# A graph-network kernel on one core: 64 narrow edge-count windows in place of 32, one incidence tile of four built on ScalarE, VectorE's work in another order

## The chip, the core and the metric

The kernel runs on one core of one Trainium2 chip, in one launch. The metric is the device time of the whole execution in microseconds (us). The engines are TensorE (PE in the profile, its weight loads PEld), VectorE (DVE), ScalarE (ACT), GpSimd (POOL) and SyncE (SP), which only issues transfers. Each engine runs its own program in order, and semaphores tie them together.

## What is computed

A node table x (1024 x 128), 32768 edges (src, dst) sorted by dst, and 64 numbers for each edge. Two layers, each ahead of it a layer norm and a relu:

```python
# layer 1: h = relu(layernorm(x))
nodes_i, nodes_j = h[src], h[dst]
messages = mlp3(concat([nodes_i, nodes_j, edge_attr]))       # 320 -> 256 -> 256 -> 128
summed = segment_sum(messages, src, N) + segment_sum(messages, dst, N)
x = x + mlp3(concat([h, summed, attention(h)]))              # 384 -> 256 -> 256 -> 128
# layer 2: h = relu(layernorm(x)); every node has a loop to itself as well
deg = segment_sum(1, col);  norm = rsqrt(deg)[row] * rsqrt(deg)[col]
out = segment_sum(norm[:, None] * (h @ W)[row], col) + b
x = x + gelu(out)
```

## The kernel before, in words

**Edges.** 32768 edges are 256 tiles of 128 edges, or 64 groups of 4 tiles. All stages of a group run in a software pipeline: in its step g each engine works on parts of the groups g - 1, g and g + 1. `run_groups` writes out the steps -1 to 64, one after the other, on each engine.

**TensorE, step g** (`group`, L677 to L698): `second_layer(g, 0)` and `second_layer(g, 1)` (L607, 6 matmuls of 512 columns each), `first_layer(g + 1)` (L587, 4 matmuls for the edge numbers, then L593, for each half k four transposes that add the gathered rows to the two banks), between its halves `scatter(g - 1, 0)` (L628, 4 matmuls), `messages(g)` (L617), and `scatter(g - 1, 1 to 3)` (L628). The transposes of tiles 0 and 1 in the first half wait for the first `add_pair` of VectorE, those of tiles 2 and 3 for the second. `scatter` multiplies the messages (high and low part) with an incidence matrix `inc` (128 edges x 1024 nodes), so that both segment sums of the reference come in one product.

**The incidence matrix** of a tile is |node - (src + dst)/2| == |src - dst|/2, times 2 for a loop edge. ScalarE's `distance` (L812) writes the left side to `dist` (f16), VectorE's `incidence` (L1005) compares and writes `inc` (fp32r). For tiles 0 and 2 (`IN_ROWS`) both have the shape of 3 rows of 342 on one side, for 1 and 3 one run of 1024.

**GpSimd** gathers for every tile one row per edge from each of two tables (L446, L454), 8 transfers for a group, into one of 3 buffers. VectorE adds the two in pairs of tiles (`add_pairs`, L1048).

**High and low parts.** After each product ScalarE writes the rounded high part (`relu_first` L796, `high_messages` L819, `round_edges` L825), and VectorE the rest (`low_first` L985, `low_messages` L991, `low_edges` L979). `relu_second` is L802 on ScalarE.

**Edge counts for layer 2.** `ct_sb` (1024 x 1024 counts) is made in `NW` = 32 windows of `WD` = 32 target nodes. As dst is sorted, a window's edges lie in a few tiles: `VT` = 10 are always done. For each of them VectorE writes two one-hot matrices, `oh_low` (L1056, 128 columns) and `oh_key` (L1057, 258 columns as 3 rows of 86 at a pitch of 88), and TensorE multiplies them (L646, `count_tile`, put between the transposes). A window takes two groups, 5 tiles in each. Then ScalarE copies it to `ct_sb` (L853, `window_out`), and VectorE sums it in both directions (`window_sums`, L1076, L1078). What a window has beyond 10 tiles is added by `more_windows`, a loop that always makes one visit; it stands ahead of step 63 on VectorE and within it on TensorE. After it come `count_ends` (L664), `degrees` and `add_bias_of_sums` (L672). GpSimd adds the diagonal of the loops last (L479).

**VectorE, step g** (`group`, L1008 to L1038): one-hots 0 and 1; `incidence(g - 1, 1)`; both pair sums; one-hot 2; `incidence(g - 1, 2)`; `low_edges`; `low_first(g + 1, 0)`; `incidence(g - 1, 3)`; one-hot 3; `low_first(g + 1, 1)`; one-hot 4; `incidence(g, 0)`; `low_messages(g)`; in even steps `window_sums`.

**ScalarE, step g** (L827 to L848): `round_edges(g + 2)`, `relu_second(g, 0)`, `distance(g - 1, 2)`, `relu_second(g, 1)`, `relu_first(g + 1, 0)`, `distance(g - 1, 3)`, `relu_first(g + 1, 1)`, `distance(g, 0)`, `high_messages(g)`, `distance(g, 1)`, in even steps `window_out`.

## Time and profile before

| | us |
|---|---|
| median of 3 runs | 767.0 (766.85 to 767.35) |
| the profiled execution | 765.72 |
| its span | 763.9 |

```profile
PE 736.0 (96%) x4171; PEld 619.3 (81%) x4171; DVE 729.5 (96%) x1506; ACT 524.3 (69%) x711; POOL 539.0 (71%) x533
PE   7589999999999999999999999999999999999896
DVE  7889999999999999999999999999999999999775
```

The first line is each engine's busy time, its share of the span, and its number of instructions. The other two cut the span into 40 slices: a digit is the busy share in tenths, and 9 is 90% or more. TensorE and VectorE are full from the third slice on to the last four. TensorE had its full clock in nearly all of the span (mean 0.994).

### The profile page before, as it was taken

The numbers are of one execution on the slowest core, as the hardware profiler recorded it, in microseconds if no ns is written. First come the engines' busy times: TensorE is split into PE (matmuls) and PEld (weight loads), VectorE is DVE, ScalarE is ACT, GpSimd is POOL, SyncE is SP. The second block draws the span as 40 slices with busy tenths as digits, with TensorE's granted clock in tenths as the row PEclk, the third lists the DMA queues.
The fourth block names the chain that finished last, engine by engine and source line by source line (L and its number), as shares of the span: only waits on it lengthen the run. The fifth ranks groups of instructions, "written<-read, shape, count | busy, mean of one in ns | idle before, by whom it ended". The sixth has DMA issues, their size and how long they took to land.

```text
span 763.9 us, 13342 instructions
## 1 busy us (share of the span) xinstructions
PE 736.0 (96%) x4171; PEld 619.3 (81%) x4171; DVE 729.5 (96%) x1506; ACT 524.3 (69%) x711; POOL 539.0 (71%) x533
## 2 busy tenths in 40 slices
PE   7589999999999999999999999999999999999896
PEld 6467888888888888888888888888888888888755
DVE  7889999999999999999999999999999999999775
ACT  3256777777777777777777777777777777776623
POOL 3777777777777777777777777777777777777100
PEclk9899999999999999999999999999999999999999
DMA  7534444344434444344443444434443444432000
GB/s 227 164 119 129 128 127 123 117 126 129 126 112 125 130 128 127 114 124 128 127 124 113 130 129 126 126 112 127 129 126 113 126 127 130 126 111 83 0 1 28
DMA packets 42566, 90.15 MB, mean 118 GB/s; under 512 B 11136, under 2 KB 17920, under 8 KB 42496
## 3 DMA queue, kind: packets, MB, share of 16 engines
q0 software_dynamic: 24576, 67.14, 28.6%
q1 hardware_dynamic: 17920, 22.16, 9.9%
q8 instruction: 33, 0.54, 0.3%
q14 instruction: 37, 0.30, 0.1%
HBM read 86.64 MB, written 2.62 MB: 117 GB/s over the span
## 4 chain that ended last, share of the span: by engine, by line
PE 88%; DVE 4%; POOL 3%; issue 2%; DMA 2%; ACT 1%; DVEq 0%; SPq 0%; POOLq 0%
PE bank L628 30%; PE bank L607 22%; PE bank L617 14%; PE bank L587 7%; PE bank L593 7%; PE bank L646 4%; POOL rows_sb L446 2%; POOL rows_sb L454 1%; DVE ring L1005 1%; PE bank L720 1%; DMA w_sb<-mW 1%; PE bank L765 1%; PE bank L728 1%; DMA table_a<-rows_sb 0%; PE bank L714 0%
## 5 line engine op out<-in xcount | busy, mean ns | idle before, releaser
L446 POOL DMA_INDIRECT rows_sb<-table_a,ends_i x256 | 263.5, 1029 | 82.2 <-issue 77.7
L454 POOL DMA_INDIRECT rows_sb<-table_b,ends_i x256 | 262.7, 1026 | 78.0 <-issue 78.0
L812 ACT ACTIVATE dist<-iota_h,neg_mid 128x1026 f16<-128x1026 f16 (+1 forms) x256 | 292.3, 1143 | 0.0
L1005 DVE TENSOR_SCALAR ring<-dist,half_gap,times 128x1026 fp32r<-128x1026 f16 (+1 forms) x256 | 276.4, 1081 | 1.7 <-ACT dist L812 0.6
L628 PE MATMUL bank<-ring,m_hi 128*128 128x512 f32 x512 | 172.4, 418 | 1.3 <-DVE ring L1005 1.1
L802 ACT ACTIVATE h_sb<-bank,b_sb 128x512 f32<-128x512 f32 x128 | 87.6, 684 | 122.5 <-PE bank L607 122.5
L628 PE MATMUL bank<-ring,m_lo 128*128 128x512 f32 x512 | 160.8, 395 | 0.0
L607 PE MATMUL bank<-ring,w_hi 128*128 128x512 f32 x512 | 150.0, 394 | 1.4 <-DVE ring L985 1.4
L1057 DVE TENSOR_SCALAR oh_key<-iota_h,key_f,minus_base 128x258 bf16<-128x258 f16 x321 | 128.5, 400 | 0.0
L617 PE MATMUL bank<-w_sb,h_sb 128*128 128x128 f32 x1024 | 124.8, 275 | 0.0
L593 PE MATMUL bank<-ident,rows_sb 128*128 128x128 f32 x512 | 113.7, 276 | 8.0 <-DVE rows_sb L1048 8.0
L617 PEld LDWEIGHTS bank<-w_sb,h_sb 128*128 128x128 f32 x1024 | 119.5, 192 | 0.1
L796 ACT ACTIVATE ring<-bank 128x512 fp32r<-128x512 f32 x128 | 76.7, 599 | 60.1 <-PE bank L593 55.8
L607 PEld LDWEIGHTS bank<-ring,w_hi 128*128 128x128 f32 x512 | 96.1, 188 | 24.4 <-DVE ring L985 2.0
L628 PEld LDWEIGHTS bank<-ring,m_lo 128*128 128x128 f32 x512 | 96.9, 189 | 23.2
L628 PEld LDWEIGHTS bank<-ring,m_hi 128*128 128x128 f32 x512 | 87.2, 191 | 13.9 <-DVE ring L1005 2.0
L985 DVE SCALAR_TENSOR_TENSOR ring<-bank,ring 128x512 fp32r<-128x512 f32 x128 | 87.8, 686 | 3.7 <-ACT ring L796 1.7
L593 PEld LDWEIGHTS bank<-ident,rows_sb 128*128 128x128 f32 x512 | 70.3, 142 | 20.7 <-DVE rows_sb L1048 11.2
L1056 DVE TENSOR_SCALAR oh_low<-iota_h,low_f 128x128 bf16<-128x128 f16 x321 | 84.8, 264 | 2.2 <-issue 2.1
L1048 DVE TENSOR_TENSOR rows_sb<-rows_sb 128x512 f32<-128x512 f32 x128 | 82.2, 681 | 3.7 <-DMA rows_sb<-table_b,ends_i 3.6
L607 PE MATMUL bank<-ring,w_lo 128*128 128x512 f32 x256 | 80.3, 395 | 0.0
L646 PE MATMUL bank<-oh_key,oh_low 128*128 128x258 bf16 x320 | 77.8, 275 | 0.0
(182 smaller groups left out, 628.5 us busy)
## 6 DMA issues: line engine op xcount, KB each, us to landing
e_raw<-edge_attr_t SPq DMA_DIRECT2D x128, 128.0 KB, 3.1
rows_sb<-table_a,ends_i POOLq DMA_INDIRECT x256, 2.8
rows_sb<-table_b,ends_i POOLq DMA_INDIRECT x256, 2.9
table_a<-rows_sb SPq DMA_DIRECT2D x4, 256.0 KB, 3.4
table_b<-rows_sb SPq DMA_DIRECT2D x4, 256.0 KB, 2.5
x_sb<-x SPq DMA_DIRECT2D x2, 256.0 KB, 3.2
out<-oh_key SPq DMA_DIRECT2D x4, 128.0 KB, 1.8
u_sb<-uW SPq DMA_DIRECT2D x1, 384.0 KB, 5.0
```

Of the source, the lines that this page charges most:

```text
L446: nc.gpsimd.indirect_dma_start(got[:, b, t, 0, :], None, table_a, bass.IndirectOffsetOnAxis(ap=ends_i[:, 0, tile:tile + 1], axis=0),).then ...
L454: nc.gpsimd.indirect_dma_start(got[:, b, t, 1, :], None, table_b, bass.IndirectOffsetOnAxis(ap=ends_i[:, 1, tile:tile + 1], axis=0),).then ...
L593: mm = nc.tensor.matmul(z1t_bank[k][:, t * P:(t + 1) * P], got[:, g % GB, t, 0, part], ident[:, :], start=False, stop=True, is_transpose=T ...
L607: mm = nc.tensor.matmul(z2_bank[m][:, :], w[:, k, m * P:(m + 1) * P], a[:, b, k, :], start=(n == 0), stop=(n == len(parts) - 1))
L617: mm = nc.tensor.matmul(msg_bank[:, t * D:(t + 1) * D], h2_sb[:, k, t * P:(t + 1) * P], w3_sb[:, k, :], start=(t == 0 and k == 0), stop=(k ...
L628: mm = nc.tensor.matmul(acc_bank[n][:, :], part[:, b, t, :], inc[:, t, n * HB:(n + 1) * HB], start=(is_first(g) and t == 0 and part is m_h ...
L646: mm = nc.tensor.matmul(bank[2][:, 0:KR * KN], oh_low[:, w % HOT, j, :], oh_key[:, w % HOT, j, :, 0:KN], start=(j == 0), stop=(j == VT - 1 ...
L802: nc.scalar.activation(h2_sb[:, m, :], z2_bank[m][:, :], ACT.Relu, bias=b2_sb[:, m:m + 1]).then_inc(h2_ready, 1)
L812: nc.scalar.activation(to, of, ACT.Abs, bias=neg_mid[:, bass.ds(g * GT + t, 1)]).then_inc(dist_ready, 1)
L985: nc.vector.scalar_tensor_tensor(h1_lo[:, b, k, :], z1t_bank[k][:, :], 0.0, h1_hi[:, b, k, :].bitcast(F32), ALU.max, ALU.subtract).then_in ...
L1005: nc.vector.tensor_scalar(to, of, half_gap[:, tile], times[:, tile], ALU.is_equal, ALU.mult).then_inc(inc_ready, 1)
L1057: return nc.vector.tensor_scalar(oh_key[:, slot, j, :, 0:KN], iota_h[:, 0:KR * KN].rearrange("p (r n) -> p r n", r=KR), key_f[:, bass.ds(t ...
```

## The change

- `VT` 10 to 6, `NW` 32 to 64, `WD` 32 to 16: 6 tiles to a window, one window to a group. `oh_key` is 2 rows of 64 at a pitch of 66 (128 columns), `HOT` 2 to 4 slots. TensorE does the 6 products together, between the second half of `first_layer` and `messages`. Steps -1, 0 and 1 make two windows each (12 tiles), after `low_messages`, so nothing is made ahead of step -1.
- Two windows are a pair. VectorE adds a pair to `ct_sb` (`pair_out`, in place of ScalarE's copy) and sums it (`pair_sums`), in every other step.
- `ct_sb` is cleared by ScalarE at the start (8 instructions of 1024 columns), with the diagonal copied in (2 more), in place of GpSimd's additions at the end. `more_windows` stands ahead of the steps, behind a wait for these 10. `count_ends` and `degrees` go from step 63 to step 62.
- Incidence tile 3 is made on ScalarE by three instructions: `distance`, `last_gap` (Abs), `last_incidence` (Relu), but for the last group's. Tiles 0, 1 and 2 are all in rows, but for the last group's.
- VectorE's pair sums, one-hots and incidence tiles stand in another order, and so do ScalarE's instructions.
- The bias rows (L474 on GpSimd) are added by VectorE in step 0. In the last step TensorE adds the bias of the sums first and does one half of the columns after the other.

```diff
-    VT = 10
-    NW = 32
+    VT = 6
+    NW = 64
-    KR, KN, KP = 3, 86, 88
+    KR, KN, KP = 2, 64, 66
-    HOT = 2
+    HOT = 4
-    IN_ROWS = (0, 2)
+    IN_ROWS = (0, 1, 2)
+    DT = GT - 1
...
+        FILL = 2
+        def made_in(g):
+            if g < FILL:
+                return [2 * (g + 1), 2 * (g + 1) + 1]
+            return [w for w in (g + 2 + FILL,) if w < NW]
+        def counted_in(g):
+            if 0 <= g <= FILL:
+                return [2 * g, 2 * g + 1]
+            return [w for w in (g + 1 + FILL,) if FILL < g and w < NW]
+        def summed_in(g):
+            pairs = [p for p in range(PAIRS) if 2 * p + 1 in counted_in(g - 1)]
+            return pairs[0] if pairs else None
+        LAST_SUM = NW - 1 - FILL
...
+            def count_window(w):
+                pe.wait_ge(w_hot, w + 1)
+                if w % 2 == 0:
+                    wait(pe, w_out, w // 2)
+                at = (w // 2) % 2 * PK + w % 2 * WK
+                for j in range(VT):
+                    mm = nc.tensor.matmul(bank[2][:, at:at + WK], oh_low[:, w % HOT, j, :], oh_key[:, w % HOT, j, :, 0:KN],
+                                          start=(j == 0), stop=(j == VT - 1), skip_group_check=True)
+                mm.then_inc(w_psum, 1)
+            def last_scatter(g, b):
+                pe.wait_ge(m_lo_ready, g + 1)
+                for n in range(NH):
+                    for t in range(GT):
+                        if n == 0:
+                            wait_incidence(g, t)
+                        for part in (m_hi, m_lo):
+                            mm = nc.tensor.matmul(acc_bank[n][:, :], part[:, b, t, :], inc[:, t, n * HB:(n + 1) * HB], ...
+                    mm.then_inc(sums_ready, 1)
             def group(g, b, i):
+                if g == GROUPS:
+                    add_bias_of_sums()
+                    last_scatter(g - 1, 1 - b)
+                    return
                 if nxt:
-                    first_layer(g + 1, 1 - b, i + b, 1, counts_of(g))
+                    first_layer(g + 1, 1 - b, i + b, 1)
+                for w in counted_in(g):
+                    count_window(w)
                 if now:
                     messages(g)
-                if g == LAST_W + 1:
+                if g == LAST_SUM + 1:
                     count_ends()
...
+            def clear_counts(chunks):
+                for c in chunks:
+                    nc.scalar.activation(ct_sb[:, c, :], iota_h[:, 0:N], ACT.Copy, scale=0.0).then_inc(ct_zero, 1)
+            def last_gap(g):
+                act.wait_ge(dist_ready, GT * g + GT)
+                nc.scalar.activation(dist[:, DT, 0:N], dist[:, DT, 0:N], ACT.Abs,
+                                     bias=neg_gap[:, bass.ds(g * GT + DT, 1)]).then_inc(gap_ready, 1)
+            def last_incidence(g):
+                act.wait_ge(gap_ready, g + 1)
+                wait(act, scattered, GT * g)
+                tile = bass.ds(g * GT + DT, 1)
+                nc.scalar.activation(inc[:, DT, 0:N], dist[:, DT, 0:N], ACT.Relu, bias=times[:, tile],
+                                     scale=neg_times[:, tile]).then_inc(last_inc_ready, 1)
             # ScalarE, step g
+                if past:
+                    distance(g - 1, 2)
                 if now:
                     relu_second(g, 0)
                 if past:
-                    distance(g - 1, 2)
+                    distance(g - 1, 3)
                 if now:
                     relu_second(g, 1)
+                if past and now:
+                    last_gap(g - 1)
                 if nxt:
                     relu_first(g + 1, 1 - b, 0)
-                if past:
-                    distance(g - 1, 3)
+                if past and now:
+                    last_incidence(g - 1)
                 if nxt:
                     relu_first(g + 1, 1 - b, 1)
...
             # VectorE, step g, as it is after the change
+                if steady:
+                    w = makes[0]
+                    tile0 = window_tile(w)
+                    one_hots(w, tile0, (0,))
+                if nxt:
+                    add_pair(g + 1, 0)
                 if past:
                     incidence(g - 1, 1)
+                if nxt:
+                    add_pair(g + 1, 1)
+                if pair is not None:
+                    pair_out(pair)
                 if past:
                     incidence(g - 1, 2)
+                if steady:
+                    one_hots(w, tile0, (1,))
+                if nxt:
+                    low_first(g + 1, 1 - b, 0)
                 if exists(g + 2):
                     low_edges(g + 2, b)
                 if nxt:
                     low_first(g + 1, 1 - b, 1)
+                if steady:
+                    one_hots(w, tile0, (2,))
+                if pair is not None:
+                    pair_sums(pair)
+                if steady:
+                    one_hots(w, tile0, (3,))
                 if now:
                     incidence(g, 0)
+                if steady:
+                    one_hots(w, tile0, (4, 5))
+                if now:
                     low_messages(g, b)
+                if not steady:
+                    for w in makes:
+                        one_hots(w, window_tile(w), range(VT))
+                if g == 0:
+                    biased_rows()
+                if g == GROUPS:
+                    incidence(g - 1, 3)
...
+            def pair_out(p):
+                dve.wait_ge(w_psum, 2 * p + 2)
+                counts = ct_sb[:, :, bass.ds(p * PD, PD)]
+                found = bank[2][:, p % 2 * PK:(p % 2 + 1) * PK].rearrange("p (d a) -> p a d", a=NC)
+                nc.vector.tensor_tensor(counts, counts, found, ALU.add).then_inc(w_out, 1)
             def more_windows():
-                dve.wait_ge(w_sums, NW)
+                dve.wait_ge(ct_zero, NC + 2)
```

## Rows read from the trace of the kernel before

**Rows 1.** Busy time by stretch: us, PE, PEld, DVE, ACT, POOL, clock, DMA, GB/s.
```profile
300.00:400.00 100.00, 100.00 (x582) 85.43 (x581) 99.16 (x196) 74.09 (x100) 77.15 (x76) 1.00 0.40 123
```

**Rows 2.** Timeline, TensorE, step 34: start us, us, engine, line, op, count.
```profile
403.11 0.62 PE L607 MATMUL bank<-ring,w_hi 128*128 128x512 f32 x2
...
406.82 0.27 PE L593 MATMUL bank<-ident,rows_sb 128*128 128x128 f32 x1
...
406.93 0.27 PE L646 MATMUL bank<-oh_key,oh_low 128*128 128x258 bf16 x1
...
407.15 0.25 PEld L593 LDWEIGHTS bank<-ident,rows_sb 128*128 128x128 f32 x2
...
409.19 1.95 PE L617 MATMUL bank<-w_sb,h_sb 128*128 128x128 f32 x16
...
413.78 0.62 PE L607 MATMUL bank<-ring,w_hi 128*128 128x512 f32 x2
```

**Rows 3.** Timeline, ScalarE, step 34; in brackets its idle time before and who ended it.
```profile
404.70 0.69 ACT L802 ACTIVATE h_sb<-bank,b_sb 128x512 f32<-128x512 f32 x1 [2.05 <-PE bank L607]
...
405.29 1.14 ACT L812 ACTIVATE dist<-iota_h,neg_mid 128x1026 f16<-128x1026 f16 x1
...
407.68 0.60 ACT L796 ACTIVATE ring<-bank 128x512 fp32r<-128x512 f32 x1 [0.67 <-PE bank L593]
```

**Rows 4.** Groups of instructions by shape: busy us, mean ns, idle before.
```profile
L454 POOL DMA_INDIRECT rows_sb<-table_b,ends_i x256 | 262.7, 1026 | 78.0 <-issue 78.0
...
L1005 DVE TENSOR_SCALAR ring<-dist,half_gap,times 128x1026 fp32r<-128x1026 f16 x128 | 170.5, 1332 | 0.3 <-ACT dist L812 0.3
...
L1057 DVE TENSOR_SCALAR oh_key<-iota_h,key_f,minus_base 128x258 bf16<-128x258 f16 x321 | 128.5, 400 | 0.0
...
L1056 DVE TENSOR_SCALAR oh_low<-iota_h,low_f 128x128 bf16<-128x128 f16 x321 | 84.8, 264 | 2.2 <-issue 2.1
...
L1076 DVE TENSOR_REDUCE into_part<-ct_sb 128x32 f32<-128x256 f32 x32 | 19.3, 602 | 0.1
L1078 DVE TENSOR_REDUCE from_part<-ct_sb 128x8 f32<-128x256 f32 x32 | 13.1, 409 | 0.0
```

**Rows 5.** Timeline, VectorE, step 23.
```profile
291.03 0.69 DVE L979 TENSOR_TENSOR e_parts<-e_raw,e_parts 64x512 fp32r<-64x512 f32 x1
291.75 0.69 DVE L985 SCALAR_TENSOR_TENSOR ring<-bank,ring 128x512 fp32r<-128x512 f32 x1
...
294.63 1.33 DVE L1005 TENSOR_SCALAR ring<-dist,half_gap,times 128x1026 fp32r<-128x1026 f16 x1
295.88 0.68 DVE L991 TENSOR_TENSOR m_lo<-bank,m_hi 128x512 fp32r<-128x512 f32 x1
```

**Rows 6.** Timeline, start: ScalarE's last L861, VectorE's first sum of pairs.
```profile
26.35 0.69 ACT L861 ACTIVATE uh_sb<-bank,ub_sb 128x512 f32<-128x512 f32 x1 [0.76 <-PE bank L571]
...
33.70 1.29 DVE L1048 TENSOR_TENSOR rows_sb<-rows_sb 128x512 f32<-128x512 f32 x2
...
43.46 0.69 DVE L1048 TENSOR_TENSOR rows_sb<-rows_sb 128x512 f32<-128x512 f32 x1 [2.92 <-DMA rows_sb<-table_b,ends_i]
```

**Rows 7.** Chain that ended last, in order of time: step 4's second layer.
```profile
83.19 2.80 PE bank L607 x12
```

**Rows 8.** Timeline, end: TensorE from step 63 on.
```profile
712.69 0.63 PE L607 MATMUL bank<-ring,w_hi 128*128 128x512 f32 x2
...
720.86 1.84 PE L664 MATMUL bank<-ones_col,into_part 128*128 128x1 f32 x16
...
727.80 0.74 PE L628 MATMUL bank<-ring,m_hi 128*128 128x512 f32 x2 [1.14 <-DVE ring L1005]
...
732.30 3.70 PE L714 MATMUL bank<-rows_sb,u_sb 128*128 128x512 f32 x8 [0.24 <-ACT rows_sb L870]
```

**Rows 9.** Timeline, VectorE, the one visit of `more_windows`.
```profile
714.16 0.23 DVE L1096 TENSOR_SCALAR over_f<-rows_f,visit_f 1x32 f32<-1x32 f32 x1 [1.19 <-issue]
...
718.67 0.41 DVE L1120 TENSOR_TENSOR ct_sb<-ct_sb,bank 128x256 f32 x1
```

More of the change, by code:

```diff
@@ L804, in distance @@
             def distance(g, t):
-                wait(act, inc_ready, GT * g + (t - 3))
+                if t < DT:
+                    wait(act, inc_ready, DT * (g - 1) + t + 1)
+                else:
+                    wait(act, last_inc_ready, g)
                 to, of = dist[:, t, 0:N], iota_h[:, 0:N]
-                if t in IN_ROWS:
+                if t in IN_ROWS and g < GROUPS - 1:
                     to = dist[:, t, :].rearrange("p (r n) -> p r n", r=DR)[:, :, 0:DN]
@@ L862, in _ @@
                                      bias=ub1_sb[:, m:m + 1]).then_inc(uh_ready, 1)
+            clear_counts(range(NC - 2, NC))
+            act.wait_ge(ct_zero, NC)
+            act.wait_ge(consts_pool, 7)
+            diagonal = ct_all[:, 0:(NC - 1) * (N + P)].rearrange("p (s n) -> p s n", n=N + P)[:, :, 0:P]
+            nc.scalar.copy(diagonal, ident[:, :].unsqueeze(1).broadcast_to([P, NC - 1, P])).then_inc(ct_zero, 1)
+            nc.scalar.copy(ct_all[:, (NC - 1) * (N + P):NC * N], ident[:, :]).then_inc(ct_zero, 1)
             nc.scalar.copy(w1e_hi[:, :], w1e_sb[:, :]).then_inc(w1e_hi_ready, 1)
@@ new lines, in group, with biased_rows, add_pair @@
+                if g == 0:
+                    biased_rows()
+                if g == GROUPS:
+                    incidence(g - 1, 3)
+            def biased_rows():
+                dve.wait_ge(ld_w, 16 * 12)
+                nc.vector.tensor_tensor(xb_sb[:, :, :], x_sb[:, :, :],
+                                        ub3_all[:, :].unsqueeze(1).broadcast_to([P, NC, D]), ALU.add).then_inc(xb_ready, 1)
+            def add_pair(g, half):
+                b, n = g % GB, g // GB
+                tiles = slice(2 * half, 2 * half + 2)
+                for t in (2 * half, 2 * half + 1):
+                    dve.wait_ge(ga_done[b][t], 16 * (n + 1))
+                    dve.wait_ge(gb_done[b][t], 16 * (n + 1))
+                nc.vector.tensor_tensor(got[:, b, tiles, 0, :], got[:, b, tiles, 0, :], got[:, b, tiles, 1, :],
+                                        ALU.add).then_inc(pair_added, 1)
@@ L1203, in _ @@
             dve.wait_ge(rows_ready, 1)
+            more_windows()
             dve.wait_ge(w1e_hi_ready, 1)
@@ L1207, in _ @@
             low_edges(0, 0)
-            tile0 = window_tile(0)
-            for half in range(2):
-                one_hots(0, tile0, half, range(VT // 2))
-            run_groups(dve, group, FIRST + 1, {1: count_passes, LAST_W: more_windows, LAST_W + 1: degrees})
+            run_groups(dve, group, FIRST + 1, {1: count_passes, LAST_SUM: sum_counts, LAST_SUM + 1: degrees})
             def round_counts(chunks):
```

157 lines of the change are left out of this document (52 added, 105 removed).

## Prediction

> **What bounds the kernel now.** I read the busy time by stretch first. In the middle of the run, all 100 us of a stretch of 100 us are busy on TensorE and 99.2 on VectorE, with ScalarE at 74 and GpSimd at 77, at full clock [rows 1]. So two engines share the bound, and the timelines have to say which sets the pace. On TensorE the second layer of step 34 starts at 403.11 and that of step 35 at 413.78 [rows 2]: 10.67 us for a step. Between these rows I saw no gap longer than the usual one from instruction to instruction, and the list of waits has none for TensorE in the middle. VectorE's instructions stand just as close, and ScalarE waits 2.05 us for TensorE ahead of L802 [rows 3]. So TensorE sets 10.67 and VectorE follows with almost no slack. What takes work from both can gain only if no chain through several engines is longer than a step. That chain is what I cost below. Times within a step count from the start of its second layer (step 34: 403.11).
>
> **Prices.** A VectorE instruction starts 0.08 before the one ahead of it ends (294.63 + 1.33 is 295.96, and the next starts at 295.88 [rows 5]). So an incidence tile in rows costs 1.25, a pair sum or a low part 0.60, L979 0.72 (291.03 to 291.75 [rows 5]), L1056 some 0.17, L1057 of 258 columns 0.32, and the two window reduces 0.52 + 0.33 = 0.85 [rows 4]. On ScalarE the overlap is 0.10 (404.70 + 0.69 against 405.29 [rows 3]), so a distance costs 1.04, L802 0.59, L796 0.50.
>
> **TensorE's own step.** It loses 5 count products at 0.11 each (406.82 to 406.93 [rows 2]), 0.54. It gains 6 of 128 columns. Bounds for one: 0.11 if the columns don't matter, 0.054 if they all do (128/258 of 0.109). I take 0.055, since the pitch of the 258-column product is just 258 columns long, which leaves no sign of a fixed part: 0.33. The own step becomes 10.67 - 0.54 + 0.33 = 10.46, or 10.79 by the upper bound. (The Trainium skill, page "TensorE: Matmul & The Clock Gate", section "Back-to-back issue gap", gives 81 ns for a stream of 128-column products with their weight loads. No row here shows one. By it the step would be 10.62, and it speaks against the change.)
>
> **VectorE's own step.** The narrower L1057 has the 128 columns of L1056. Its pitch lies between 0.17 (that row's) and 0.32 (no change). I take 0.21, near the lower end, since only one scalar operand sets it apart: a one-hot costs 0.38, bounds 0.34 and 0.49. Two steps hold 6 incidence tiles 7.50, 4 pair sums 2.40, 4 `low_first` 2.40, 2 `low_edges` 1.44, 2 `low_messages` 1.20, 12 one-hots 4.56, `pair_out` 0.33 (256 elements like L1078) and the reduces 0.85: 20.7, or 10.3 a step. It has slack of its own. (By "VectorE: DVE Perf Modes", section "What auto-detection actually checks" of the Trainium skill, two ports serve an instruction if the outermost counts of both sides are even or equal. The old L1057 writes 3 rows and doesn't qualify, the new one writes 2 and does. That agrees with a shorter L1057, but those ports are shared with GpSimd, see the fourth rival.)
>
> **ScalarE** gets two more instructions of 1.04 a step and loses half of L853. It was 74% busy [rows 1], that is 7.9 us of a step, so it goes to some 9.8 and fits. But it does the new work ahead of results others wait for.
>
> **The chain.** Second layer starts at 0; L802 starts at 1.59 (404.70 [rows 3]); then, in program order, distance 3 at 2.18, `relu_second` 1 at 3.22, `last_gap` 3.81, `relu_first` 0 at 4.85, `last_incidence` 5.35, `relu_first` 1 at 6.39 to 6.99. (Before, `relu_first` 0 started at 4.57 [rows 3], set by the transposes.) The new instructions are bounded by 0.9 and 1.15 each; I take the distance's 1.04. Then VectorE goes on with `low_first` 1: 0.60, one-hot 0.38, reduces 0.85, one-hot 0.38, incidence 0 1.25, two one-hots 0.76, `low_messages` 0.60, in the next step one-hot 0.38, pair sum 0.60, incidence 1 1.25, second pair sum 0.68: 7.73, end at 14.7. The transposes of tiles 2 and 3 wait for that sum. Their weights were loaded at 407.15, 4.04 into the step [rows 2]; without two counts ahead of them it is 3.82, so 3.82 + 10.46 = 14.28 in the next step. The sum comes 0.45 late and TensorE stands. From there it needs 10.46 - 3.82 = 6.64 to the next second layer, at 21.4. In the step without reduces the sum ends 0.85 earlier and is in time. Two steps take 21.4, one takes 10.69, against 10.67 before. So the 0.21 that TensorE's own step gains is eaten, and what is late next is the second pair sum. With the bounds for counts and one-hots the step is 10.6 to 11.1.
>
> **The start.** Ahead of step -1 stood 10 one-hots (4.8 us, up to the first pair sum at 33.70 [rows 6]). Now `more_windows` stands there, behind ScalarE's clears. The last L861 starts at 26.35 [rows 6]; two clears and two diagonal copies (1.04 twice, an estimated 1.2 for both copies) end at 30.3. The visit costs 1.19 of issue, 714.16 to 718.67, less two reduces of 0.34, plus 0.41 [rows 9] and 0.3 to its end: 5.7. With L1205 (0.4) and L979 VectorE is free at 37.0, not at 33.7, and the second layer of step 0 starts at about 42.5 (it takes 5.5 from there, at a clock that has fallen while TensorE idled; a guess of 0.5 either way). Then VectorE carries 12 one-hots (4.55) in each of the steps -1, 0 and 1 where it had 5. In order: step -1 ends on it at 47.0; step 0 (pair sums 1.2, a wait of 1.1 for ScalarE, low parts 2.0, incidence and `low_messages` 1.85, one-hots 4.55, bias rows 1.15) at 58.9; step 1 (13.3, and 1.1 for `count_passes`) at 73.4; step 2, with a pair, at 84.4; the second pair sum of step 3 at 87.3. So step 4's second layer starts at 94.0, where it was 83.19 [rows 7]: **10.8 late**. Before, VectorE had waited here for gathers (2.92 us at 43.46 [rows 6]), which is gone as cover now: GpSimd is ahead by then. Bounds: 8 (one-hot 0.34, visit 5) to 14.
>
> **The middle.** 56 steps from 4 to 60 at +0.02: +1. Steps 60 to 62 have no one-hots on VectorE and run at TensorE's own 10.46, 10.13 and 10.13 + 1.79 for `count_ends` (L664, 16 matmuls, 1.84 with its tail [rows 8]). That is 32.5 against some 32.3: +0.2, with 0.4 more for the disturbed step 62 of before. I count +0.6, so step 63 starts 12.4 later than at 712.69 [rows 8].
>
> **The end.** Before, from 712.69 to the update's first matmul at 732.30 [rows 8] it was 19.6, with the visit, `count_ends`, a wait of 1.14 for incidence and the bias behind. Now from 0: second layer to 2.8, scatter to 3.7, messages 3.9 to 5.7, scatter to 8.5, bias 1.0 to 9.5. ScalarE's distance 3 of the last group ends at 10.8 and VectorE's fast tile at 11.6; then 10 matmuls of 0.235 after it: 14.0. So **-5.6**. The two edits that cost nothing here: the order of halves (it only lets ScalarE copy earlier) and the diagonal, which ScalarE does in the start.
>
> **Sum**, against the profiled execution's own 765.7: +10.8 + 1.0 + 0.6 - 5.6 = +6.8, 772.5. The median of the runs shown lies 1.3 higher, so I forecast 773.8, **774**.
>
> **The rivals.** About 0.2% is what a measurement of this kernel can tell from no change.
> 1. *TensorE's own step sets the pace* (faster). If the chain is shorter than 20.9 instead of 21.4 (one-hots at 0.34 give 0.2, new ScalarE instructions at 0.9 give 0.4), the 56 steps run at 10.46: 56 x 0.21 = 11.8 less than at 10.67, and 774 - 12.9 = 761. For it: two engines get less work. Against: VectorE's order, with reduces between `low_first` 1 and the pair sums. It decides from a chain of 20.9 on, and is in sight for all below 21.2. Chance 0.22.
> 2. *The count products cost as much as before*, 0.11: the part behind the pair sum grows by 0.33, two steps take 21.7, 56 x 0.16 more, 783. Against: the pitch follows columns elsewhere. Chance 0.12.
> 3. *The start costs half*: if the clears are through early or the long one-hot runs fit into waits, 4 to 6 us less, 769, or 767 with a chain a little shorter. Chance 0.12.
> 4. *GpSimd becomes the bound.* A gather takes 1.026 + 0.30 [rows 4], 8 of them 10.6 a step, with VectorE's fast instructions in their way. The fast incidence tiles go, 7 short one-hot instructions come. Only above 10.9 a step would it matter, since it is a buffer or two ahead: 785 at 10.9. Chance 0.04.
>
> **How the numbers follow.** The forecast has 0.50, on 770 to 780. Slower by over 0.2%: forecast 0.50, rivals 2 and 4 0.16, a part of 3, together 0.70. Within 0.2%: 0.08, from 3. Faster: 0.22. The range reaches from rival 1 to rival 2: 760 to 784.
>
> **What would show it.** In the changed kernel's profile: TensorE waits at L593 for the pair sum in every other step, 0.3 to 0.6 each time, and two steps take 21.2 to 21.6; the second layer of step 4 starts near 94; VectorE has a wait ahead of `low_first` in steps with a pair; count products follow each other by 0.055; the update starts 14 us after step 63. Wrong would be: no wait on TensorE in the middle (rival 1), or a step 4 that starts below 90.

## The result, and the profile after

| | before | after |
|---|---|---|
| median, us | 766.92 (4 runs) | 782.06 (4 runs, 781.32 to 783.39) |
| the profiled execution | 765.72 | 781.32 |
| its span | 763.9 | 779.6 |
| ratio of the medians, 95% interval | | 1.020 (1.018 to 1.022) |

The kernel got 15.1 us slower; I had forecast 6.8 slower, with 784 as the upper end of the range. The page of the kernel after, busy time and slices:

```profile
PE 737.6 (95%) x4235; PEld 617.2 (79%) x4235; DVE 725.4 (93%) x1601; ACT 645.7 (83%) x815; POOL 539.6 (69%) x530
PE   7486999999999999999999999999999999999996
DVE  7689999999999999999999999999999999998665
PEclk9878999999999999999999999999999999999999
```

Two places show already. In slices two to four TensorE is at 4, 8 and 6 tenths and its granted clock at 8, 7 and 8, and in the middle, by stretch (the view of [rows 1]), TensorE is no longer full:

```profile
300.00:400.00 100.00, 98.82 (x574) 83.47 (x574) 97.85 (x211) 89.83 (x112) 77.31 (x75) 1.00 0.42 124
```

TensorE's timeline over two steps, the counterpart of [rows 2]:

```profile
421.00 0.63 PE L611 MATMUL bank<-ring,w_hi 128*128 128x512 f32 x2
...
425.38 0.44 PE L599 MATMUL bank<-ident,rows_sb 128*128 128x128 f32 x2 [0.27 <-DVE rows_sb L1112]
...
427.02 0.50 PE L651 MATMUL bank<-oh_key,oh_low 128*128 128x128 bf16 x6
427.36 2.00 PE L621 MATMUL bank<-w_sb,h_sb 128*128 128x128 f32 x16
...
431.97 0.63 PE L611 MATMUL bank<-ring,w_hi 128*128 128x512 f32 x2
...
442.51 0.63 PE L611 MATMUL bank<-ring,w_hi 128*128 128x512 f32 x2
```

One step takes 10.97 and the next 10.54, and in the longer one the transposes of tiles 2 and 3 wait for the second sum of pairs (L1112). The six count products take 0.34 together. The chain that leads to this wait starts one step earlier, in the step with the reduces (TensorE and VectorE):

```profile
410.47 0.63 PE L611 MATMUL bank<-ring,w_hi 128*128 128x512 f32 x2
...
417.54 0.69 DVE L1029 SCALAR_TENSOR_TENSOR ring<-bank,ring 128x512 fp32r<-128x512 f32 x1 [0.20 <-ACT ring L821]
...
424.64 0.68 DVE L1112 TENSOR_TENSOR rows_sb<-rows_sb 128x512 f32<-128x512 f32 x1
```

Here `low_first` 1 starts 7.07 after the second layer, the second sum of the next step ends 7.78 after that (425.32), and 6.65 later the next second layer starts (431.97). ScalarE in the longer step (the counterpart of [rows 3]):

```profile
422.60 0.69 ACT L827 ACTIVATE h_sb<-bank,b_sb 128x512 f32<-128x512 f32 x1 [0.97 <-PE bank L611]
423.19 1.14 ACT L840 ACTIVATE dist<-iota_h,neg_mid 128x1024 f16<-128x1024 f16 x1
424.22 0.68 ACT L827 ACTIVATE h_sb<-bank,b_sb 128x512 f32<-128x512 f32 x1
424.79 1.14 ACT L846 ACTIVATE dist<-dist,neg_gap 128x1024 f16<-128x1024 f16 x1
425.86 0.60 ACT L821 ACTIVATE ring<-bank 128x512 fp32r<-128x512 f32 x1
426.35 1.23 ACT L855 ACTIVATE ring<-dist,times,neg_times 128x1024 fp32r<-128x1024 f16 x1
427.48 0.59 ACT L821 ACTIVATE ring<-bank 128x512 fp32r<-128x512 f32 x1
```

That is the order of the forecast's chain; `last_incidence` (L855) has a pitch of 1.13 where I had 1.04. The list of waits of the kernel after (us in total, times, the longest):

```profile
PEld bank L599 <- DVE rows_sb L1112: 25.0, 32, 4.7
DVE ring L1029 <- ACT ring L821: 17.3, 45, 2.4
```

Where the time lies, by the start of each step's second layer:

| | before | after | change |
|---|---|---|---|
| step 4 | 83.03 | 97.78 | +14.75 |
| steps 4 to 60 | 597.45 (10.669 a step) | 603.35 (10.774) | +5.9 |
| steps 60 to 63 | 32.21 | 32.72 | +0.5 |
| step 63 to the end of the span | 51.2 | 45.73 | -5.4 |

The start, by stretch (the columns of [rows 1]), in the kernel after:

```profile
37.00:43.00 6.00, 4.00 (x13) 3.12 (x14) 3.55 (x7) 1.70 (x3) 4.53 (x5) 0.50 0.47 139
43.00:48.00 5.00, 5.00 (x12) 3.88 (x13) 5.00 (x25) 0.69 (x1) 3.78 (x5) 0.50 0.51 159
...
61.00:66.00 5.00, 3.84 (x16) 2.93 (x17) 4.62 (x6) 1.76 (x3) 4.09 (x4) 0.53 0.27 78
```

From 43 to 48 TensorE was busy all the time at a granted clock of 0.50, the lower level of 1.2 GHz: it had idled 8.25 us up to 34.76 and 2 us each up to 37.0 and 42.76. The second layer of step 0 took 5.3 us there, where that of step 34 took 2.8. (Up to step 4 the clock was at 0.50 from 32 to 48, from 59 to 65 and from 80 to 82; in the kernel before from 32 to 38 alone.) After an idle time of 4.3 us up to 60.96 the clock was at 0.53 again. The end went as the forecast had it: the update's first matmul comes 14.2 after step 63, where it was 19.6 after it [rows 8].

### The profile page after: what moved, and what is told of

Same layout as the page of the kernel before. It is cut to its first block, busy times and chain, and to the rows that moved or that the text cites. A ratio compares the mean times of both kernels' runs of the same rounds, so it can differ in the third digit from the quotient of the medians.

```text
span 779.6 us, 13796 instructions
## 1 busy us (share of the span) xinstructions
PE 737.6 (95%) x4235; PEld 617.2 (79%) x4235; DVE 725.4 (93%) x1601; ACT 645.7 (83%) x815; POOL 539.6 (69%) x530
## 4 chain that ended last, share of the span: by engine, by line
PE 68%; DVE 21%; issue 6%; ACT 3%; DVEq 1%; POOL 0%; POOLq 0%
PE bank L639 25%; PE bank L621 14%; PE bank L611 12%; PE bank L599 7%; DVE ring L1049 5%; DVE rows_sb L1112 5%; PE bank L593 4%; DVE oh_low L1120 3%; PE bank L651 3%; DVE oh_key L1121 2%; DVE m_lo L1035 2%; ACT dist L840 1%; PE bank L737 1%; PE bank L782 1%; ACT ring L821 1%
## 5 line engine op out<-in xcount | busy, mean ns | idle before, releaser
L470 POOL DMA_INDIRECT rows_sb<-table_b,ends_i x256 | 272.6, 1065 | 78.0 <-issue 78.0
L462 POOL DMA_INDIRECT rows_sb<-table_a,ends_i x256 | 260.0, 1016 | 82.7 <-issue 77.4
L1049 DVE TENSOR_SCALAR ring<-dist,half_gap,times 128x1026 fp32r<-128x1026 f16 (+1 forms) x193 | 255.5, 1324 | 6.3 <-ACT dist L840 6.2
L1121 DVE TENSOR_SCALAR oh_key<-iota_h,key_f,minus_base 128x128 bf16<-128x128 f16 x385 | 131.7, 354 | 0.0
L621 PE MATMUL bank<-w_sb,h_sb 128*128 128x128 f32 x1024 | 128.1, 278 | 0.1
L1029 DVE SCALAR_TENSOR_TENSOR ring<-bank,ring 128x512 fp32r<-128x512 f32 x128 | 88.2, 689 | 21.2 <-ACT ring L821 17.3
L599 PE MATMUL bank<-ident,rows_sb 128*128 128x128 f32 x512 | 85.4, 281 | 16.9 <-DVE rows_sb L1112 16.9
L1120 DVE TENSOR_SCALAR oh_low<-iota_h,low_f 128x128 bf16<-128x128 f16 x385 | 99.1, 258 | 1.8 <-issue 1.8
L599 PEld LDWEIGHTS bank<-ident,rows_sb 128*128 128x128 f32 x512 | 64.7, 144 | 42.8 <-DVE rows_sb L1112 25.0
L639 PEld LDWEIGHTS bank<-ring,m_hi 128*128 128x128 f32 x504 | 86.2, 191 | 11.3
L1112 DVE TENSOR_TENSOR rows_sb<-rows_sb 128x512 f32<-128x512 f32 x128 | 87.0, 681 | 0.0
L855 ACT ACTIVATE ring<-dist,times,neg_times 128x1024 fp32r<-128x1024 f16 x63 | 78.0, 1238 | 0.0
```

Source lines behind the costliest of these rows:

```text
L462: nc.gpsimd.indirect_dma_start(got[:, b, t, 0, :], None, table_a, bass.IndirectOffsetOnAxis(ap=ends_i[:, 0, tile:tile + 1], axis=0),).then ...
L470: nc.gpsimd.indirect_dma_start(got[:, b, t, 1, :], None, table_b, bass.IndirectOffsetOnAxis(ap=ends_i[:, 1, tile:tile + 1], axis=0),).then ...
L599: mm = nc.tensor.matmul(z1t_bank[k][:, t * P:(t + 1) * P], got[:, g % GB, t, 0, part], ident[:, :], start=False, stop=True, is_transpose=T ...
L621: mm = nc.tensor.matmul(msg_bank[:, t * D:(t + 1) * D], h2_sb[:, k, t * P:(t + 1) * P], w3_sb[:, k, :], start=(t == 0 and k == 0), stop=(k ...
L639: mm = nc.tensor.matmul(acc_bank[n][:, :], part[:, b, t, :], inc[:, t, n * HB:(n + 1) * HB], start=(is_first(g) and t == 0 and part is m_h ...
L1029: nc.vector.scalar_tensor_tensor(h1_lo[:, b, k, :], z1t_bank[k][:, :], 0.0, h1_hi[:, b, k, :].bitcast(F32), ALU.max, ALU.subtract).then_in ...
```

## Experiments

The first four tell three explanations of the middle apart and test the clock. C is my forecast's chain; V says that VectorE itself is full; G says that the gathers on GpSimd bound the step.

**e1: both sums of pairs together.**

```diff
+                if nxt:
+                    add_pair(g + 1, 1)
                 if past:
                     incidence(g - 1, 1)
-                if nxt:
-                    add_pair(g + 1, 1)
```

> The kernel after, with VectorE's second sum of pairs moved ahead of incidence tile 1, so that both sums stand together. Both theories say that TensorE's wait of some 0.5 us for that sum in every other step goes away, since the sum ends 1.25 us earlier. Theory C (the chain of my forecast: only the chain through ScalarE, low_first 1 and the second sum makes two steps 21.54 long): the chain is 1.25 shorter, TensorE's own 10.53 sets the step, 56 steps gain 0.24 each, 13 us in all, some 769. Theory V (VectorE is full: of 21.54 us in two steps only some 0.2 are waits, so that its own work is 21.3, 10.67 a step, and not the 20.7 that I forecast): the wait of TensorE only moves or shrinks, VectorE's waits for relu_first go, and the step falls to about 10.67: 56 x 0.1 = 6 us less, some 776. Mean step: C 10.53, V 10.65 to 10.70.

Measured: 771.1, ratio to the kernel before 1.0052 (1.0036 to 1.0069), mean step 10.63. That fits neither C nor V, and the mean hides why. From step 4 to 20 a step takes 10.507, just what C says; from 20 to 60 it takes 10.68. VectorE was 99.3% busy from 100 to 200 us, yet ran at 10.507, so V falls. In the later part a wait stands in the list that the kernel after doesn't have:

```profile
DVE rows_sb L1112 <- DMA rows_sb<-table_b,ends_i: 8.6, 21, 2.2
```

I followed the lead of the gathers, from the end of a group's last gather to its second sum: in e1 11.9 us at group 5, 8.4 at 8, 5.9 at 12, 2.9 at 16, 2.1 at 20, and about 2 from there on. In the kernel after it stands at 16.3 through the whole middle, in the kernel before at 3.1. So while e1's lead lasted, the gathers took 11.17 us a group (from the end of group 5 to that of group 20); once VectorE waited for them, both ran at 10.68.

**e2: `relu_first` 1 ahead of `last_incidence`.**

```diff
-                if past and now:
-                    last_incidence(g - 1)
                 if nxt:
                     relu_first(g + 1, 1 - b, 1)
+                if past and now:
+                    last_incidence(g - 1)
```

> The kernel after, with ScalarE's relu_first 1 ahead of last_incidence: the 1.13 us of last_incidence leave the chain to low_first 1, and VectorE's waits for relu_first (33 of them, 6.6 us) should go. Theory C: the chain of two steps is 1.1 shorter, the step falls to TensorE's own 10.53, some 769. Theory V: only these waits can be won, 0.1 a step, mean step 10.65 to 10.70, some 776. Rival: nothing is won, since incidence tile 3 then comes too late for scatter 3, and TensorE waits there: mean step 10.77, 782.

Measured: 777.3, 1.014 (1.0123 to 1.0157), mean step 10.69, 10.68 in every part. Not 10.53, so the link that I took out of the chain has come in at another place. ScalarE now waits 0.6 or 0.3 us for TensorE ahead of `relu_first` 1 (6.06 and 5.75 into steps 40 and 41), so that `distance(g, 0)` starts 0.7 and 0.45 later than in the kernel after (7.69 and 7.37, where it had 6.97 and 6.92), and VectorE's incidence tile 0 waits for it.

```profile
DVE ring L1049 <- ACT dist L840: 15.2, 35, 4.6
```

In the kernel after this line has 6.2 us in 5 times. So ScalarE's order does bear on the step, as C has it, but both ends of it feed VectorE. The step agrees with V's number too; e1 and f2 are what rules V out. In e2 the gathers' lead shrinks as well, from 15.8 us at group 5 to 2.0 at group 60: they took 10.9 a group, and only the end of the steps kept them from setting the pace.

**e3: incidence tile 1 in one run.**

```diff
-    IN_ROWS = (0, 1, 2)
+    IN_ROWS = (0, 2)
```

> The kernel after, with incidence tile 1 in one run of 1024 columns in place of 3 rows of 342, as it was before. In the kernel before this form had a pitch of about 0.73 us where the rows have 1.25, so VectorE gets 0.5 us a step back, on its own step and on the chain. Theories C and V both say that VectorE falls to about 10.15 a step and TensorE's 10.53 sets it: mean step 10.53, some 769. Theory G (the form in one run stands in GpSimd's way, and with the short one-hots the gathers become the bound): GpSimd's L462 and L470, 1.065 us in the mean, rise beyond 1.09, no step gains, and TensorE or VectorE wait for gathers: 780 or more.

Measured: 770.6, 1.0053 (1.0032 to 1.0073), mean step 10.59: 10.52 up to step 20, 10.62 behind. It repeats e1 by another edit: VectorE gets 0.5 us a step back (94% busy from 300 to 400), the step falls to TensorE's own, and then VectorE waits for gathers, 19.8 us in 21 times.

**e4: TensorE kept busy at the start.**

```diff
+                        if g in (2, 3):
+                            pe.wait_ge(m_lo_ready, g - 1)
+                            keep_busy({(2, 0): 36, (2, 2): 8, (3, 0): 15, (3, 2): 10}[g, t], bank[7])
...
+                    if g == 0:
+                        keep_busy(14, bank[7])
...
+            keep_busy(60, bank[7])
             more_windows()
+            keep_busy(14, bank[7])
```

> The kernel after, with matmuls of 128 columns on TensorE that nobody reads (157 in all, each some 0.11 us at the full clock), put where it idles at the start: ahead of more_windows, of step -1, of step 0's second layer, and ahead of the transposes in steps 1 and 2. Nothing else is changed. Theory K (of the 4 us that the start cost beyond my sum, the clock that fell while TensorE idled is the cause: 43 to 48 us went by at half clock, a second layer of 5.3 in place of 2.8, and again 61 to 65 and 79 to 81): with the clock kept the second layer of step 4 starts 3 to 4 us earlier than at 97.8, the whole takes 778 to 779. Rival S (VectorE alone sets the start, and the half clock lies beside its work): step 4 moves by under 1 us, 781 to 782.

Measured: 790.3, 1.0306 (1.0289 to 1.0323). The clock was 1.00 throughout, but the edit did more than it was meant to: an unread matmul stands in the profile as two of 0.112 us and not one, so the first 60 lasted 13.6 us where 8.25 had been idle, and held TensorE up. It decides nothing on the clock; f1 repeats it with half.

**f1: the same, half as many.**

> As e4, with half as many unread matmuls in each place (30, 7, 7, then 18 and 4, then 7 and 5), since each of them took two passes of 0.112 us there, 0.22 in all, twice what I had counted with, and so they themselves held TensorE up: step 4 came at 105.8. Now they last 6.7 and 1.6 us at the start and 4.0, 0.9, 1.6, 1.1 later, each less than the idle time that stood there. Theory K (the fallen clock costs 3 to 4 us of the start): second layer of step 4 near 94.5, the whole 778 to 779. Rival S (VectorE sets the start, the half clock lies beside it): step 4 at 97 to 98, the whole 781 to 782.

Measured: 777.2, 1.0132 (1.0115 to 1.0149), step 4 at 93.77: 4.0 us earlier than in the kernel after. The same stretches as above:

```profile
43.00:48.00 5.00, 3.49 (x18) 2.46 (x17) 4.38 (x19) 1.47 (x3) 4.08 (x4) 1.00 0.42 124
...
61.00:66.00 5.00, 5.00 (x43) 4.59 (x43) 4.94 (x8) 4.03 (x6) 3.86 (x4) 1.00 0.39 118
```

With the clock at 1.00 the start comes to the time that I had worked out (94.0), and the steps are still 10.77. K holds: these 4.0 us are the fallen clock's, 1.25 of them ahead of step 0's second layer (41.51 for 42.76) and 2.76 between it and step 4. The half clock didn't lie beside VectorE's work alone: in the kernel after VectorE was full from 43 to 48, but then had nothing to do for 1.85 us up to 50.49, as ScalarE waited for TensorE's late transposes.

**f2: e1 with seven gathers of eight.**

```diff
                 for t in range(GT):
                     gather_a(g, t)
-                    gather_b(g, t)
+                    if t < GT - 1:
+                        gather_b(g, t)
```

> As e1 (both sums of pairs together), with the last of the eight gathers of each group from 1 on left out: it leaves out the second table's rows for tile 3, so that its sum takes whatever the buffer holds. VectorE's and TensorE's instructions are those of e1. In e1 the steps took 10.51 up to step 20 and 10.67 from there on, when the gathers had used up their lead (from 12 us to 2). Theory G (the gathers, prolonged by VectorE's instructions beside them, are the bound of e1's later steps): with one in eight gone, 10.51 holds up to step 60, 40 steps by 0.16, 6 to 7 us less than e1's 771.1: 764 to 765. Rival V (VectorE's own work, 10.67 a step): no change, 771.

(VectorE's sum of tiles 2 and 3 doesn't wait for the one left out.) Measured: 764.7, 0.9972 (0.9961 to 0.9983), 10.507 in every part up to step 60. VectorE's and TensorE's work is e1's, and 6.4 us are gone. So G holds for e1's later steps, and V is out.

**f3: without the visit.**

```diff
-            more_windows()
+            dve.wait_ge(ct_zero, NC + 2)
```

(and without `more_windows()` on TensorE)

> The kernel after without the one visit of more_windows on VectorE and TensorE (what windows have beyond 6 tiles is left out); VectorE still waits for ScalarE's clears where the visit stood. The visit lasts from 31.2 to 35.5. If the start is VectorE's work in a row, as my sum had it, all of 4.3 us comes off: second layer of step 0 at 38.5 in place of 42.8, of step 4 at 93.5, the whole 777 to 778; 1 to 2 us more if TensorE's clock falls less. Rival: the gathers' data are late then (in the kernel before VectorE waited 2.9 us for them here), and only 2 us come off: 780.

Measured: 776.25, 1.0123 (1.0106 to 1.014). Step 0 starts at 37.6 and step 4 at 91.9, 5.9 earlier. Of these 5.1 are there at VectorE's first sum of pairs already (31.74 for 36.88): the visit with its issue costs that, not 4.3. The other 0.8 come behind step 0, where TensorE's clock is back at 1.00 from 36 us on and not from 49. VectorE waited for a gather once, 0.3 us.

**f4: FILL = 1.**

```diff
-        FILL = 2
+        FILL = 1
```

> The kernel after with FILL = 1: two windows are made in the steps -1 and 0 only, and the last window one step later, with count_ends in step 63 in place of 62. Six one-hots, 2.3 us of VectorE, go from step 1 to step 60. If VectorE's work sets the start (my sum), step 4 starts 2.3 earlier, near 95.4; step 60 takes 0.2 to 0.4 more, and count_ends (1.8) goes from step 62 to 63, ahead of the last step, which moves nothing in sum: 780. Rival: the wait only moves to step 2, and the whole stays at 782.

Measured: 777.1, 1.0131 (1.0113 to 1.0149), step 4 at 93.78. I expected 2.3 us and 4.0 came: with six one-hots less ahead of it, step 2's first sum starts at 72.92 and not at 76.10, TensorE's two idle times of 1.86 and 1.41 go, and with them the fall of its clock there (0.66 from 79 to 84 in the kernel after, 1.00 here).

**g1: the order of e1 in every other step.**

```diff
+                if nxt and pair is None:
+                    add_pair(g + 1, 1)
                 if past:
                     incidence(g - 1, 1)
-                if nxt:
+                if nxt and pair is not None:
                     add_pair(g + 1, 1)
```

> The kernel after, with the two sums of pairs together in the steps without pair_out only, those in which TensorE waits for the second sum; in the others incidence tile 1 stays between them. Theory C (the chain): TensorE's wait goes as in e1, and the step is 10.51 to 10.53, 14 us less than 782: 768. Theory G (gathers that fall behind once they meet the sums) splits it: if the order of half the steps leaves the gathers as they are in the kernel after (they keep a lead of 16 us there), 10.52 holds to the end; if the gathers take their 10.66 here as in e1, the steps go from 10.51 to 10.67 after some 20 steps, and the whole is 771.

Measured: 771.4, 1.0049 (1.0031 to 1.0067). 10.507 up to step 30, then 10.61 to 10.71: the lead of the gathers starts at 16 us and is down to 2.8 at group 30. The second branch of what I expected.

**g3: the kernel before with the last step of the kernel after.**

```diff
+                if g == GROUPS:
+                    add_bias_of_sums()
+                    last_scatter(g - 1, 1 - b)
+                    return
```

> The kernel before with the last step of the kernel after alone: the bias of the sums ahead of the last scatter, and that one half of the columns after the other, so that ScalarE copies the first half while TensorE makes the second. The counts, the visit and count_ends stay where they were in step 63. Of the 5.4 us that the end gained, this part should give the 1.0 us of the bias, which now lies in the 1.14 us that TensorE waits for incidence tiles, and at most 1 more for the copy: 765 to 766. The other 3.5 to 4.4 us then belong to the visit and count_ends, which the kernel after took out of step 63. Rival: the bias has to wait for degrees on VectorE, and nothing is gained: 767.

Measured: 766.3, 0.9995 (0.9985 to 1.0004): nothing, where I had expected 1 to 2. The bias does fill the wait for the incidence tiles, but the matmuls behind the last tile are then ten and not four, 2.4 us in place of 0.9 and the bias of 1.0 behind them. The update starts 19.5 after step 63 (19.6 before), but this one trace can't be set against that of the kernel before: its clock was at 0.50 from 719 to 723, where the other had 1.00, and the same matmuls took 1.6 us longer. The medians decide, over 12 and 23 executions: by their interval the edit gives 1.2 us at most. So at least 4 of the 5.4 us of the end are not this edit's. By subtraction they belong to the visit and `count_ends`, which the change took out of step 63.

**g4: three edits together.** The order of g1, `FILL = 1`, and the unread matmuls of f1 in the five places where TensorE still idled (30, 7, 7, 18 and 5).

> The kernel after with three edits that the earlier runs priced: the order of g1, FILL = 1 as in f4, and the unread matmuls of f1 at the places that still idle (30, 7, 7, 18, 5). If the start is made of parts that add, step 4 comes 4.0 + 4.0 earlier less what both take from the same half clock: near 91. With the steps at 10.52 as theory C has them, 782 - 14 - 6.5 = 761 to 762, below the kernel before. If theory G holds for this order too, the gathers set the end, whatever the start gains: 768 to 771.

Measured: 766.5, 1.0004 (0.999 to 1.0018). Step 4 starts at 90.4, as expected. The steps take 10.533 up to step 20 and 10.69 behind, so of the 14 us that the order should give only a part came. In e1, e3, g1 and g4 alike the gathers take over, whatever gave the slack.

**What prolongs a gather.** An undisturbed gather took 0.95 us and the next started 0.30 later: 8 of them are 10.0 a group, which would bound nothing. But some take longer, up to 1.55 in the kernel after and 2.1 in e1. GpSimd and VectorE in the kernel after, two timelines of one stretch:

```profile
403.25 1.34 POOL L470 DMA_INDIRECT rows_sb<-table_b,ends_i  x1 [0.30 <-issue]
404.90 0.95 POOL L462 DMA_INDIRECT rows_sb<-table_a,ends_i  x1 [0.30 <-issue]
406.15 1.40 POOL L470 DMA_INDIRECT rows_sb<-table_b,ends_i  x1 [0.30 <-issue]
...
412.95 1.55 POOL L462 DMA_INDIRECT rows_sb<-table_a,ends_i  x1 [0.30 <-issue]
```

```profile
403.10 0.67 DVE L1112 TENSOR_TENSOR rows_sb<-rows_sb 128x512 f32<-128x512 f32 x1
403.70 1.33 DVE L1049 TENSOR_SCALAR ring<-dist,half_gap,times 128x1026 fp32r<-128x1026 f16 x1
...
406.04 0.69 DVE L1023 TENSOR_TENSOR e_parts<-e_raw,e_parts 64x512 fp32r<-64x512 f32 x1
...
413.00 0.68 DVE L1112 TENSOR_TENSOR rows_sb<-rows_sb 128x512 f32<-128x512 f32 x1
```

The three ends are 403.77, 406.73 and 413.68, and the three gathers end 0.82, 0.82 and 0.82 later. I counted this over all gathers of the middle of the kernel after (438 between 100 and 690 us), by the VectorE instruction that runs 0.13 us after the gather's start (0.13 is the 0.95 of an undisturbed gather less the 0.82), and where two overlap by the later one:

| at that point | gathers | mean, us | longest |
|---|---|---|---|
| a sum of pairs (L1112) | 56 | 1.41 | 1.55 |
| `low_edges` (L1023) | 30 | 1.40 | 1.44 |
| incidence in rows (L1049) | 136 | 0.96 | 1.04 |
| one-hots (L1120, L1121) | 110 | 0.95 | 1.01 |
| low parts with an operand in PSUM (L1029, L1035) | 54 | 0.95 | 0.95 |
| nothing, or a reduce | 52 | 0.95 | 0.97 |

Seen from the other side, 113 of the 438 took over 0.97 us. 80 of these ended 0.82 after a sum of pairs, among them the 26 longest of the row on L1049, and 30 ended 0.82 after a `low_edges`. So an instruction with both operands in SBUF holds a gather up if it runs at that point, and the short one-hots hardly do. In the kernel before the tiles in one run (L1005, 0.8 us) held gathers as well: 84 of them, 1.09 in the mean. Another 27 gathers of that kernel, of 1.17 us with a 258-column one-hot over their start, fit none of this, and what held them is open. The Trainium skill, page "SBUF — State Buffer", section "SBUF: two separate sides", has one pair of ports shared by VectorE and GpSimd as an exclusive lock, taken by a VectorE instruction in a two-port mode or, against a GpSimd instruction that reads SBUF, with two inputs in SBUF. The gather reads its indices `ends_i` there, and the sums (1.41 in the mean) and `low_edges` (1.40) agree. The rows add that a gather is held at one point, so that order and phase decide what it costs. That these ports are the reason is not shown by a run.

**h1: one-hots between the two sums.** That gives a remedy to try. In e1 two sums in a row hold for 1.28 us, longer than the 1.25 from gather to gather, so that one of them is always caught.

```diff
-                    one_hots(w, tile0, (0,))
                 if nxt:
                     add_pair(g + 1, 0)
-                if past:
-                    incidence(g - 1, 1)
+                if steady:
+                    one_hots(w, tile0, (0, 1))
                 if nxt:
                     add_pair(g + 1, 1)
+                if past:
+                    incidence(g - 1, 1)
```

(one-hot 1 goes from its old place; FILL = 1 and the unread matmuls as in g4)

> As g4 (FILL = 1, the unread matmuls at the start), with another order on VectorE in every step: first sum of pairs, one-hots 0 and 1, second sum, incidence tile 1. The second sum ends 0.87 us earlier than in the kernel after, enough for the 0.5 that TensorE waited. In all runs so far a gather took 0.95 us, but one whose point 0.13 us after its start fell into a sum of pairs or a low_edges waited for the end of that instruction and took 0.82 from there. Theory P (that hold is the price of the gathers): with 0.77 us of one-hots, which hold nothing, between the sums, two sums no longer block 1.28 us in a row, the gathers' period falls below the 10.67 to 10.76 of e1 and g4, toward 10.55, and the whole comes to 760 to 763. Rival: the gathers take 10.67 and more whatever the order, since each step has the same three holding instructions: 766 to 768.

Measured: 759.7 (759.46 to 761.37), 0.9902 (0.9885 to 0.9919): 7 us faster than the kernel before and 22 faster than the kernel after. Its middle by stretch, and that of g4:

```profile
500.00:600.00 100.00, 100.00 (x583) 85.07 (x583) 99.32 (x220) 90.32 (x115) 76.81 (x77) 1.00 0.43 127
```

```profile
500.00:600.00 100.00, 99.79 (x592) 84.89 (x591) 98.63 (x212) 90.86 (x115) 76.85 (x77) 1.00 0.42 126
```

The steps take 10.53 up to step 60, the lead of the gathers stays at 9.4, and a gather takes 1.010 in the mean where g4's takes 1.042. Not fewer take over 0.97 us (108 in h1, 96 in g4, by the count above), but each is held for less: those that end behind a sum take 1.28 in place of 1.40, those behind a `low_edges` 1.12 in place of 1.33. Between g4 and h1 only VectorE's order differs, and it is worth 7 us.

Where the second layer starts, and the length of a step, in all runs (from TensorE's timelines):

| | step 4 | a step, 4 to 20 | a step, 20 to 60 | median |
|---|---|---|---|---|
| before | 83.0 | 10.67 | 10.67 | 766.9 |
| after | 97.8 | 10.78 | 10.77 | 782.1 |
| e1 | 95.8 | 10.51 | 10.68 | 771.1 |
| e2 | 97.6 | 10.68 | 10.69 | 777.3 |
| e3 | 95.3 | 10.52 | 10.62 | 770.6 |
| e4 | 105.8 | 10.79 | 10.79 | 790.3 |
| f1 | 93.8 | 10.78 | 10.77 | 777.2 |
| f2 | 96.0 | 10.51 | 10.51 | 764.7 |
| f3 | 91.9 | 10.77 | 10.77 | 776.25 |
| f4 | 93.8 | 10.78 | 10.77 | 777.1 |
| g1 | 99.6 | 10.51 | 10.62 | 771.4 |
| g3 | 84.0 | 10.67 | 10.67 | 766.3 |
| g4 | 90.4 | 10.53 | 10.69 | 766.5 |
| h1 | 92.2 | 10.52 | 10.53 | 759.7 |

The columns of steps come from one execution each, and up to step 4 they depend on when its clock fell: g1 differs up to there from the kernel after in the place of one sum alone and reads 99.6, with the clock at 0.50 from 79 to 85. The 4.0 us of f1 and of f4 each rest on such a pair of traces; their medians, 4.9 below that of the kernel after, bear them out.

## Why the forecast had the right sign and half the size

The four terms of the sum were +10.8, +1.0, +0.6 and -5.6. They measured +14.75, +5.9, +0.5 and -5.4.

- **The mechanism of the middle was right.** The second sum of pairs is late in every other step, TensorE waits for it and for nothing else, and the step between is its own. e1 takes the wait away by moving that sum alone.
- **The middle term was mis-sized: 21.55 for two steps in place of 21.4.** The forecast's chain was 7.0 to `low_first` 1, 7.73 to the end of the second sum, and 6.64 to the next second layer. In the mean of 27 pairs of steps these parts took 7.07, 7.81 and 6.67. I had priced `last_incidence` like a distance, 1.04; it has 1.13. A one-hot was 0.385, for 0.38. TensorE's own step is 10.507 (e1, f2) and not 10.46; that does not lengthen a pair of steps that the chain sets, but it leaves less to win. None of these is large, but the term stood on a difference of 0.02 between two numbers of 10.7, and over 56 steps an error of 0.09 came to 4.9 us.
- **The start was mis-sized, in the step "it takes 5.5 from there, at a clock that has fallen while TensorE idled; a guess of 0.5 either way".** I had the fallen clock for step 0's beginning only (42.5, measured 42.76). It stayed at 0.50 to 48 and fell again behind each idle time that VectorE's 12 one-hots made. The term missed 4.0. f1 prices the fallen clock at 4.0 too, but the two are not the same: 1.25 of f1's lie ahead of step 0, where the forecast had the fallen clock in, and 2.76 behind, where it hadn't. The rest of the miss is spread over step 0, 0.26 late for its own reasons, and 0.76 of the work from there up to step 4 (52.3 us in f1 for 51.5); the last 0.16 is step 4 of the kernel before, 83.03 on TensorE's timeline for 83.19. That f1's 93.8 meets the 94.0 is in part luck. f3 and f4 price the visit at 5.9 (forecast 5.7; 5.1 without the clock) and the six one-hots of the sixth window at 4.0, with their shares of the clock.
- **The end was right** (-5.6, measured -5.4). I had counted the bias, now ahead of the last scatter, as a part of it; g3 shows that the last step's new order as a whole brings 1.2 us at most, so that the term comes for the most part from what left step 63.
- **Count products**: 0.34 for six, as forecast; rival 2 (0.11 each) is out. Rival 3 (half the start) is out.
- **Rival 1** named the gain from a shorter chain as 56 x 0.21 and a step of 10.46. The chain can be shortened by an edit of one line (e1), and 10.51 came, but for 16 steps only: a bound stood behind it that rival 1 did not have.
- **Rival 4** named the right engine, GpSimd, with 10.6 a group and a bound from 10.9. In the kernel after it indeed bounds nothing, with a lead of 16 us; f1, f3 and f4 have the same middle with leads of 10.0, 11.3 and 13.3, and the same 10.77. But I blamed the wrong instructions: the one-hots hardly hold a gather, and the sums of pairs and `low_edges`, which both kernels have, do. And it matters from some 10.7 on, as soon as the step falls below, and not only above 10.9.

What stays open: why the gathers keep a fixed lead of 16.3 in the kernel after and 9.4 in h1, where they could run ahead to the limit of their buffers (in e4 they reach it, with a lead of 18.8 and waits for TensorE's transposes, and a step of 10.79). That they are held at a point of their own and so fall in step with VectorE's order fits the rows, and the four different leads under one order as well, but no run was made for it. Nor was the lead itself set on purpose. The end's 5.4 is assigned to the visit and `count_ends` by subtraction alone.

## What to carry to other kernels

Where a forecast rests on a chain that is within a per cent of the step before, price each link from its own kind of row, and give the bound of the step for the engine that comes next: here three engines lay within 0.3 us (TensorE 10.51, the chain 10.77, the gathers 10.68 in e1), and each edit only handed the bound on. Extra work at the start can cost more than its own length if TensorE idles beside it and resumes at the lower clock: 4.0 us of the start were the clock's here. Read the lead of a prefetching queue over the run, not the mean: a mean step of 10.63 was 10.51 until the lead was used up and 10.68 from there.

## What the runs showed of the hardware

- A gather on GpSimd (0.95 us) that meets, 0.13 us after its start, a VectorE instruction with both operands in SBUF or one that writes fp32r from f16 in one long run ends 0.82 after that instruction (110 of the 113 long gathers of the kernel after). Two sums in a row made single gathers of 2.1 us in e1. Placing 0.77 us of one-hots between them took a mean gather from 1.042 to 1.010 us, and the kernel from 766.5 (g4) to 759.7 (h1).
- Unread matmuls in TensorE's idle times kept the granted clock at 1.00 where it had been 0.50 to 0.66, for 4.0 us of 780 (f1). Each 128x128 f32 matmul of this kind stands in the profile as two of 0.112 us, and twice as many of them (e4) made the kernel 8 us slower than the kernel after.
- `last_incidence`, a Relu on ScalarE from f16 to fp32r with two operands per partition, takes 1.24 us for 1024 columns, where `last_gap`, an Abs from f16 to f16 with one, takes 1.14. No run tells which of these differences makes the 0.1.
